# Cross-attention with a mixture of experts: the context read by columns, the keys stored without padding

## The reference

```python
x = x + tanh(g_xattn) * xattn(layernorm(x), ctx_2048, Wq, Wkv, null_kv, Wout, ln_scale, ln_bias)
x = x + tanh(g_ffn) * ffn(layernorm(x), ...)      # 1 shared and 32 routed experts, 8 of them for a token

def xattn(x, context, ...):
    q = split_heads(x @ Wq) * 64 ** -0.5
    k, v = split(context @ Wkv)                   # Wkv is 512 x 2048
    k = concat(null_kv[0], k); v = concat(null_kv[1], v)      # one null key and value: 78 columns of scores
    out = softmax(q @ k.T) @ v                    # for each batch and head
    return layernorm(out @ Wout) * ln_scale + ln_bias
```

## Time and profile before

| what | value |
| --- | --- |
| device times of the 3 runs | 2190.7, 2192.11, 2195.33 us |
| the profiled execution, first to last instruction | 2192.8 us |
| PE busy | 2063.8 us (94%) |
| DVE, ACT, POOL busy | 1808.0, 1417.6, 1217.7 us |
| DMA, mean of the 16 engines | 313 GB/s, 687.31 MB |

### The profile page before, as it was taken

One profiled execution on the slowest core, in us unless ns is written; L12 is line 12 of the kernel. 1 busy time (PEld: TensorE's weight loads), 2 busy tenths in 40 slices (PEclk: granted clock), 3 DMA queues, 4 the chain that ended last, 5 costly groups with the idle time before them and its releaser, 6 DMA issues. The chain is left out here.

```text
span 2192.8 us, 44099 instructions
## 1 busy us (share of the span) xinstructions
PE 2063.8 (94%) x14386; PEld 1908.0 (87%) x14386; DVE 1808.0 (82%) x4258; ACT 1417.6 (65%) x4098; POOL 1217.7 (56%) x1326
## 2 busy tenths in 40 slices
PE   8899789899999999999998689999999999999994
PEld 7888679899999999999998578888888888888884
DVE  5655447889999999999998676767999999999996
ACT  4433257667777777777775337777777777777761
POOL 1000301677777777777777620005777777777775
PEclk9999879999999999999998899999999999999997
DMA  9998768988888888888887899999999999999997
GB/s 314 318 312 296 267 211 288 304 291 269 275 265 266 267 267 270 273 274 268 267 269 249 276 375 290 284 287 346 403 403 397 397 393 392 388 400 396 392 363 271
DMA packets 393519, 687.31 MB, mean 313 GB/s; under 512 B 136875, under 2 KB 257420, under 8 KB 390828
## 3 DMA queue, kind: packets, MB, share of 16 engines
q1 hardware_dynamic: 344140, 550.21, 73.3%
q0 software_dynamic: 49152, 134.28, 16.9%
HBM read 345.89 MB, written 338.43 MB: 312 GB/s over the span
## 5 line engine op out<-in xcount | busy, mean ns | idle before, releaser
L1704 POOL DMA_INDIRECT parts<-results_dram,kept_index x512 | 517.9, 1011 | 381.0 <-DMA results_dram<-y 218.2
L853 POOL DMA_INDIRECT pages_dram<-rows,kept_index x512 | 516.2, 1008 | 171.5 <-issue 139.2
L932 ACT ACTIVATE exps<-sim,minus_max 128x78 f32<-128x78 f32 x1024 | 321.6, 364 | 53.1 <-DVE minus_max L1029 53.1
L932 ACT ACTIVATION_READ_ACCUMULATOR exps<-sim,minus_max 128x1 f32 x1024 | 250.1, 244 | 0.0
L1725 ACT ACTIVATE w_h<-w_raw 128x768 fp32r<-128x768 f32 x159 | 134.0, 843 | 151.1 <-DMA w_raw<-in_experts 150.9
L1813 DVE SCALAR_TENSOR_TENSOR parts<-parts,kept_weight 128x256 f32<-128x256 f32 x448 | 214.2, 478 | 3.3 <-DMA parts<-dense_dram 2.2
L1787 DVE TENSOR_TENSOR w_l<-w_raw,w_h 128x768 fp32r<-128x768 f32 x159 | 151.7, 954 | 41.2 <-ACT w_h L1725 40.8
L1910 PE MATMUL xps<-ident,xin 128*128 128x128 f32 x1272 | 167.0, 274 | 17.9 <-DVE wq_l L1775 8.5
L139 PE MATMUL yps<-w_h,hid_h 128*128 128x256 f32 x636 | 179.6, 282 | 2.2 <-DVE hid_l L1870 2.0
L141 PE MATMUL yps<-w_l,hid_h 128*128 128x256 f32 x636 | 178.6, 281 | 0.0
L140 PE MATMUL yps<-w_h,hid_l 128*128 128x256 f32 x636 | 178.2, 280 | 0.0
(11 more groups left out here) (272 smaller groups left out, 7312.0 us busy)
## 6 DMA issues: line engine op xcount, KB each, us to landing
xin<-pages_dram SPq DMA_DIRECT2D x159, 512.0 KB, 10.7
results_dram<-y SPq DMA_DIRECT2D x159, 512.0 KB, 9.6
w_raw<-in_experts SPq DMA_DIRECT2D x159, 385.0 KB, 9.4
pages_dram<-blank SPq DMA_DIRECT2D x108, 512.0 KB, 3.4
keys_h_dram<-keys_h SPq DMA_DIRECT2D x32, 624.0 KB, 5.0
keys_l_dram<-keys_l SPq DMA_DIRECT2D x32, 624.0 KB, 6.6
kT_h<-keys_h_dram SPq DMA_DIRECT2D x32, 624.0 KB
kT_l<-keys_l_dram SPq DMA_DIRECT2D x32, 624.0 KB
```

Of the source, the lines that this page charges most:

```text
L853: pool.indirect_dma_start(dram["pages"], bass.IndirectOffsetOnAxis(ap=kept_index[:, at:at + 1].bitcast(U32), axis=0), buffer(batch)[:, k / ...
L932: last = act.activation(exps[u % 2][:, h, :], scores(u)[:, h // 4, h % 4, :], ACT.Exp, bias=minus_max[u][:, h:h + 1], accum_out=row_sum[u] ...
L1704: pool.indirect_dma_start(parts[slot(batch, t)][:, k, :], None, done, bass.IndirectOffsetOnAxis(ap=kept_index[:, at:at + 1].bitcast(U32), ...
```

## The change

The context comes laid out by columns: the input is `ctxT`, [4 groups, 128 partitions, 4 chunks, 616 rows], instead of `ctx`. The tiles are loaded as 128 x 4 x 128 numbers into `ctx_cols`, and ACT and DVE split them from there into `ctxT_h` and `ctxT_l`. PE's transposes (L500) and their PSUM banks go: the banks turn over the 26 names of `PRODUCTS`. The places of C0 to C4 in the order of ACT, DVE and SP stay. K00 now waits for C2 instead of C3. The first piece of weights is split behind C2 of the first group, ahead of its C3.

A key's eviction is one instruction over 128 partitions. The keys' tile holds 77 columns for a pair, no zeros and no null key, and four pairs; a batch of keys in DRAM is 128 x 616 numbers instead of 128 x 1248. In the attention stage, `kT` gets its zeros (POOL) and its null columns (ACT, DVE) once at the start, and a load of keys is two DMAs a part, each of 64 partitions x 8 pieces of 77 numbers.

```diff
+PRODUCTS = [n for n in CRING if n[0] != "C"]
 CBANK = 8
 PIECE, STAGES = 1024, 4
 COLS = PIECE // CC
-CTURN = -(-len(CRING) // CBANK) * CBANK
-KPART = 2
+CTURN = -(-len(PRODUCTS) // CBANK) * CBANK
+KPART = 4
...
-    rows = sb("ctx_rows", [P, CTILES, CTX])
+    ctx_cols = sb("ctx_cols", [P, CC, CROWS])
     ctxT = [sb(f"ctxT_{s}", [P, CC, CROWS], F32R) for s in "hl"]
-    keys = [[sb(f"keys{i}_{s}", [P, CBATCHES, KPART, 2 * J], F32R) for s in "hl"] for i in range(KSLOTS)]
-    null_k = sb("null_k", [P, 1])
+    keys = [[sb(f"keys{i}_{s}", [P, CBATCHES, KPART, M], F32R) for s in "hl"] for i in range(KSLOTS)]
...
-        return banks[CRING.index(name) % CBANK]
+        return banks[PRODUCTS.index(name) % CBANK]
...
-            def load_rows(t, g):
-                sp.dma_start(rows[0:size(t), t, :], ctx_rows[g * CROWS + t * P:g * CROWS + t * P + size(t), :]).then_inc(rows_loaded[t], 16)
+            def load_columns(t, g):
+                sp.dma_start(ctx_cols[:, :, columns(t)], dram["ctxT"][g, :, :, columns(t)]).then_inc(cols_loaded[t], 16)
...
-            with nc.allow_non_contiguous_dma(reason="one column of 64 elements"):
-                for half, _ in halves:
-                    sp.dma_start(null_k[half, :], dram["null_kv"][0:1, :].rearrange("a d -> d a")).then_inc(null_loaded, 16)
...
-                        first = int(name[2]) // KPART * KPART * 2 * J
+                        first = int(name[2]) // KPART * KPART * M
                         sp.wait_ge(lo, at(CRING, name, g))
                         for out, tile in zip(keys_out, keys[unit % KSLOTS]):
-                            sp.dma_start(out[:, g * CG + i * CBATCHES:g * CG + (i + 1) * CBATCHES, first:first + KPART * 2 * J],
-                                         tile[:, :, :, :].rearrange("p b q j -> p b (q j)").bitcast(F32)).then_inc(keys_stored[unit % KSLOTS], 16)
+                            sp.dma_start(out[:, g * CG + i * CBATCHES:g * CG + (i + 1) * CBATCHES, first:first + KPART * M],
+                                         tile[:, :, :, :].rearrange("p b q m -> p b (q m)").bitcast(F32)).then_inc(keys_stored[unit % KSLOTS], 16)
...
-                            sp.wait_ge(full, at(CRING, name, g))
-                            load_rows(t, g + ahead)
+                            sp.wait_ge(lo, at(CRING, name, g))
+                            load_columns(t, g + ahead)
...
-            for slot in keys:
-                for tile in slot:
-                    last = pool.memset(tile[:, :, :, :].rearrange("p b q j -> p (b q j)").bitcast(F32), 0.0)
-            last.then_inc(keys_zeroed, 1)
...
-                    act.wait_ge(full, at(CRING, name, g))
+                    if name[0] == "C":
+                        t, of = int(name[1]), g if name == "C4" else g + 1
+                        act.wait_ge(cols_loaded[t], 16 * (of + 1))
+                        if of:
+                            act.wait_ge(full, at(PRODUCTS, f"V{t}1", of - 1))
+                        signal(act.activation(ctxT[0][:, :, columns(t)], ctx_cols[:, :, columns(t)], ACT.Copy))
+                        if name == "C2" and g == -1:
+                            split_high(0)
+                        if name == "C4" and g == 0:
+                            for i in range(CC, 2 * CC):
+                                split_high(i)
+                        continue
+                    act.wait_ge(full, at(PRODUCTS, name, g))
                     ps = bank(name)
                     if name[0] == "K":
                         pair, unit = int(name[2]), key_unit(name, g)
                         if pair % KPART == 0 and unit >= KSLOTS:
                             act.wait_ge(keys_stored[unit % KSLOTS], 32 * (unit // KSLOTS))
-                        for half, col in halves:
-                            last = act.activation(keys[unit % KSLOTS][0][half, :, pair % KPART, col:col + M],
-                                                  ps[half, 0:CCOLS].rearrange("p (b m) -> p b m", m=M), ACT.Copy)
-                    elif name[0] == "V":
+                        last = act.activation(keys[unit % KSLOTS][0][:, :, pair % KPART, :],
+                                              ps[:, 0:CCOLS].rearrange("p (b m) -> p b m", m=M), ACT.Copy)
+                    else:
...
-                    else:
-                        t = int(name[1])
-                        last = act.activation(ctxT[0][:, :, t * P:t * P + size(t)],
-                                              ps[:, :].rearrange("p (c r) -> p c r", c=CC)[:, :, 0:size(t)], ACT.Copy)
                     signal(last)
-                    if name == "C4" and g == 0:
-                        for i in range(CC, 2 * CC):
-                            split_high(i)
...
             step(-1)
-            for i in range(CC):
+            for i in range(1, CC):
                 split_high(i)
-
-            act.wait_ge(null_loaded, 32)
-            act.wait_ge(keys_zeroed, 1)
-            for slot in keys:
-                for half, col in halves:
-                    last = act.activation(slot[0][half, :, :, col + M], null_k[half, 0:1].unsqueeze(2).broadcast_to([DH, CBATCHES, KPART]), ACT.Copy)
-            last.then_inc(null_hi, 1)
...
-                        last = dve.tensor_tensor(ctxT[1][:, :, t * P:t * P + size(t)],
-                                                 ps[:, :].rearrange("p (c r) -> p c r", c=CC)[:, :, 0:size(t)],
-                                                 ctxT[0][:, :, t * P:t * P + size(t)].bitcast(F32), ALU.subtract)
-                    elif name[0] == "K":
-                        for half, col in halves:
-                            high, low = (tile[half, :, int(name[2]) % KPART, col:col + M] for tile in keys[key_unit(name, g) % KSLOTS])
-                            last = dve.tensor_tensor(low, ps[half, 0:CCOLS].rearrange("p (b m) -> p b m", m=M), high.bitcast(F32),
-                                                     ALU.subtract)
+                        signal(dve.tensor_tensor(ctxT[1][:, :, columns(t)], ctx_cols[:, :, columns(t)],
+                                                 ctxT[0][:, :, columns(t)].bitcast(F32), ALU.subtract))
...
+                        high, low = (tile[:, :, int(name[2]) % KPART, :] for tile in keys[key_unit(name, g) % KSLOTS])
+                        last = dve.tensor_tensor(low, ps[:, 0:CCOLS].rearrange("p (b m) -> p b m", m=M), high.bitcast(F32),
+                                                 ALU.subtract)
...
-                    if i < len(CRING) and made_in(CRING[i], step):
-                        pe.wait_ge(lo, at(CRING, CRING[i], step))
+                    if i < len(PRODUCTS) and made_in(PRODUCTS[i], step):
+                        pe.wait_ge(lo, at(CRING, PRODUCTS[i], step))
...
-                    if name[0] == "C":
-                        ahead = 0 if name == "C4" else 1
-                        pe.wait_ge(rows_loaded[i], 16 * (g + ahead + 1))
-                        for c in range(CC):
-                            last = pe.transpose(ps[:, c * P:c * P + size(i)], rows[0:size(i), i, c * P:(c + 1) * P],
-                                                ident[0:size(i), 0:size(i)])
-                    elif name[0] == "K":
+                    if name[0] == "K":
                         if name[2] == "0":
-                            pe.wait_ge(lo, at(CRING, "C4", g) if i else at(CRING, "C3", g - 1))
+                            pe.wait_ge(lo, at(CRING, "C4", g) if i else at(CRING, "C2", g - 1))
...
+    halves = [(slice(0, DH), 0), (slice(DH, P), J)]
+
+    def null_keys():
+
+        return [null_k[half, 0:1].broadcast_to([DH, PAIRS]) for half, _ in halves]
...
         def load_keys(batch):
             for part, name in zip(kT, ("keys_h", "keys_l")):
-                sp.dma_start(part[:, :, :].rearrange("p q j -> p (q j)").bitcast(F32), dram[name][batch]).then_inc(keys_loaded, 16)
+                of_batch = dram[name][batch].rearrange("p (q m) -> p q m", m=M)
+                for half, col in halves:
+                    sp.dma_start(part[half, :, col:col + M].bitcast(F32), of_batch[half, :, :]).then_inc(keys_loaded, 16)
...
         sp.dma_start(null_v[:, :], dram["null_kv"][1:2, :]).then_inc(null_loaded, 16)
+        with nc.allow_non_contiguous_dma(reason="one column of 64 elements"):
+            for half, _ in halves:
+                sp.dma_start(null_k[half, :], dram["null_kv"][0:1, :].rearrange("a d -> d a")).then_inc(null_k_loaded, 16)
         load_keys(0)
...
         pool.wait_ge(made, 3)
+        for part in kT:
+            for (half, _), (_, col) in zip(halves, reversed(halves)):
+                last = pool.memset(part[half, :, col:col + J].bitcast(F32), 0.0)
+        last.then_inc(keys_zeroed, 1)
+        pool.wait_ge(keys_zeroed, 1)
...
             if b == -2:
                 act.wait_ge(null_loaded, 16)
```

(18 more changed lines are left out.)

42 lines of the change are left out of this document (21 added, 21 removed).

## The result

The changed kernel takes 2157.45 us (median of 4 runs, 2156.68 to 2162.15) against 2191.4 us (2183.43 to 2195.33) for the kernel before: a ratio of 0.9847, 95% interval 0.9823 to 0.987. That is 34 us less, clear of the scatter though under 2%; 21 were forecast. Several of the runs further down, on two other chips, took 2736 to 2916 us, the kernel before with them, and their whole times are compared only with each other. The profiled execution has a span of 2156.4 us, 36.4 less than before.

What follows compares the result with a forecast made beforehand. PE was taken to bound the steady attention batches and, less cleanly, the context stage. Context -21.9, start of attention +2.5 and early batches -1.5 gave -20.9 us: span 2171.9, forecast 2171 us, range 2162 to 2181.

Steps and rivals of the forecast that it cites:

- steady batches: The 24 later attention batches: PE-bound at 27.75 us each, expected to stay unchanged.
- Context stage: Stage before attention: earlier start, no transposes, fewer waits for stores and context tiles, in sum -21.9 us.
- K0: Key products of context group 0: without transposes, 30.74 becomes 28.9 us, 1.8 less.
- V0: Value products of context group 0: fewer transposes and bank waits, 37.6 becomes 29.4 us, 8.2 less.
- K1: Key products of context group 1: the clock stays up, 29.4 to 26.9 us, 2.5 less.
- V1: Value products of context group 1: no transposes and no wait for C3, 31.5 to 27.9 us.
- Rival 1: Context stage: the stall only changes its name, as late stores of values still hold banks; 2181 us, chance 0.16.
- Start of attention: Start of the attention stage: added memsets and issues delay PE by 2.5 us, bounds +1 and +5.
- rival 4: Start of attention costs 6 us more, as batch 1's keys stand as 2048 pieces behind a fill; 2177, chance 0.08.
- Early batches: Five early attention batches, bound by transfers: cheaper key loads give -1.5 us (-5.5 to +6.5).
- Rival 2: Early batches: key loads at the unloaded price, -5.5 us, and earlier fills take as much again; 2163, chance 0.12.
- Rival 3: Every attention batch: small pieces make key loads late, slower than before, 2249 us at 75 ns a piece; chance 0.04.

Runs made afterwards that it cites:

- e18: Changed kernel with the null key's tile allocated last, so operands keep their earlier distance from the weights, at full clock: 2167.91 us against 2189.34 for the kernel before.
- e8: Changed kernel with three tiles of values and two of keys, and the zeros of `kT` behind those of the values: 2865.04 us, ratio 1.0012.
- e9: Kernel before with an unused tile ahead of `wq` and `wo`, moving weights and operands together by 32 bytes: 2190.69 us against 2189.11.
- e17: Kernel before with one unused tile that moves the operands alone 32 bytes further from the weights, at full clock: 2180.38 us against 2189.34.
- e1: Kernel before with one unused tile moving the attention operands by 32 bytes, with standstills of PE: ratio 1.0041 (0.9979 to 1.0102).
- e6: Changed kernel with the null key's tile allocated last, in a run with standstills of PE: 2846.31 us against 2855.25 for the kernel before.

## Why the prediction was wrong

The direction and the largest term held, the range (2162 to 2181) did not. The step that failed is "PE bounds it, and nothing in the change takes work from PE there", which put the steady batches at 0: they gave 6.4 us, by where the new tile `null_k` pushes the operands. The change without that shift (e18: 2167.91 us, with the kernel before at 2189.34) lies inside the range.

- Context stage, forecast -21.9, measured -21.9, the tenth by luck as said above. First product 10.8 us (11.4 forecast), K0 28.8 (28.9), V0 30.2 (29.4), K1 27.3 (26.9), V1 27.8 (27.9), K2 27.2 (26.9). The start gave 0.6 more, V0 and the K windows together about as much less. V0 varies from run to run (28.0 in e18). Rival 1 had the mechanism partly right, a wait for a bank remains (2.2 us, once), but it keeps no more than that. ACT's waits for stores of values came to 17.8 us, where under 15 was the sign. The earlier trace rows was misread a little: of its 6,406 pieces 5,135 are of 1248 bytes, and they take 61 ns, not 65.
- Start of attention, forecast +2.5, measured +0.5; rival 4 (+6) fell. The step that failed here: "So the delay reaches PE". `v_main` went out 2.6 us later behind the start of the stage, the keys of batch 1 only 1.1, and PE's scores 0.5; e8 shows the same of an earlier `v_main`, whose gain SP's later issues take up. PE waited 7.1 us at batch 1 (forecast 6 to 9), for 7.93 in the earlier trace rows:

```profile
295.23 0.47 PE L140 MATMUL sim<-kT_h,qT_h 128*128 128x156 f32 x1 [7.08 <-issue]
```

- Early batches, forecast -1.5, measured -6.3 (-5.1 without the place). The mis-sized term is the price of a load of keys, 0.7 us less in these batches instead of 0.3. The new load was sized well: 3.2 to 3.3 us measured, 3.5 as the middle of 2.3 and 4.7, and 25 to 26 ns for a piece of 308 bytes stand between the two rows (18.2 and 36.9), not at an end. The old load was undersized: 3.9 to 4.1 us measured, where the middle of 3.4 and 4.2 was 3.8. Six loads are 4.3 us; how they come to 4.9 in the fifth batch is argued, not shown: with less in the queue the fills may land sooner. Rival 2 (p 0.12) had the direction, but not its unloaded price, and its -9.5 in these batches was too much. The section "Why small descriptors are slow" of the Trainium skill ("DMA: Bandwidth & Descriptors") gave an estimate of -6 us here, and the total came near it; its 35% less for a load did not come, the packets show 18% to 20%, so that agreement is luck.
- Steady batches, forecast 0, measured -6.4: the term that was missing altogether, and the largest part of the miss of 15.5 us. "Nothing in the change takes work from PE there" was true and not enough: the change moves the operands' addresses, and PE's step depends on how they stand to the weights. In spans: 2171.9 forecast, - 6.4 here - 2.3 in the stretch behind (whose cause is not shown) = 2163.2; the early batches' 4.8 and the start's 2.0 more make 2156.4, what was measured.
- Rival 3 (slower) fell: 308-byte pieces cost 26 ns, far less than 62.

## What to carry to other kernels

A change that adds, drops or resizes a tile moves the tiles behind it. Before you credit a gain or a loss of a per cent to what a change does, run the change of addresses alone, as one unused tile, and compare the step between matmuls, which can be read in any stretch at full clock. Where two bottlenecks stand in series, removing both can give more than the sum of the two alone. And where a resource is close to full, a load's price should be taken from its packets over whole batches, not from two microseconds.

## What the runs showed of the hardware

PE's step between matmuls depends on where the tile that it loads and the tile that it streams stand to each other in SBUF: 113.9 to 118.8 ns for the same product at four distances, 32 bytes apart. Which rule of the address stands behind it stays open; four distances don't settle it, and the two products don't follow one curve. In the scores and in the product with the values both tiles moved together in every run, so nothing is known of their distances. The page "TensorE: Matmul & The Clock Gate" of the Trainium skill ("Step-by-step: what each phase is for") has two independent read ports, so that a weight load takes no bandwidth from the running matmul. These runs do not fit that easily: with both tiles moved together the step is long (118.5 ns, e9), with one of them moved it is short (114.3 ns, e17).

The other is the standstill: the kernel before ran at a mean granted clock of 0.97 in 2183 to 2195 us, and at 0.86 to 0.89 in 2745 to 2906 us on two other chips. PE's busy time grows by 4.2 us a steady batch there, and 7.2 us of idle time come in ahead of instructions that wait for nothing in the profile (e1). The granted clock was at one of two levels in every record, full or half, and fell behind such a standstill, so it is not shown to be the cause; in the context stage it was the same as before (0.98 in both). What stops PE was not found. With it, a kernel that is 1% shorter at full clock (e18) was no shorter (e6: 1.0, 0.996 to 1.004); the changed kernel itself was not run so.
